# Attention loop: two PSUM banks for the accumulated heads, one for the turned probabilities, and the own block one step later

## The reference

```python
x = x + _L0_cond_ref(...)          # a 32x32 matrix per sequence, chosen by an index
x = x + _L1_cond_ref(...)          # base weight, bias and a LoRA adapter per sequence
x = x + _L2_cond_ref(...)          # attention, below
x = x + _L3_cond_ref(...)          # as the first
# _L2: HQ=32 query heads, HK=8 key heads, D=128, cache of L=512 keys per sequence
q, k, v = x @ Wq.T, x @ Wk.T, x @ Wv.T ; q, k = rope(rmsnorm(q)), rope(rmsnorm(k))
k_all = concat(k_cache[block_table], k)      # 512 + 32 keys
v_all = concat(v_cache[block_table], v)
probs = softmax(where(valid, q @ k_all.T * SCALE, -1e30))
return (probs @ v_all) @ Wo.T
```

## Time and profile before

| | |
|---|---|
| Time, median of 3 runs | 2406.7 us (2405.97 to 2408.63) |
| Span of the profiled execution | 2408.5 us (the core was busy from the first to the last instruction; nothing lies around it) |
| TensorE busy, matmuls | 2319.6 us, 96% of the span |
| TensorE weight loads | 2006.1 us, 83% |
| VectorE | 1763.3 us, 73% |
| ScalarE | 1629.7 us, 68% |
| GpSimd | 1411.4 us, 59% |
| Granted TensorE clock, mean | 0.994 of full speed |

### The profile page before, as it was taken

The page is one execution under the profiler, slowest core; times in us unless marked ns, Lnnn a source line. Parts: engine busy times, 40 slices in busy tenths (PEclk is TensorE's granted clock), DMA queues, the critical chain, the costliest instruction groups (busy, mean ns, idle before and its releaser), DMA issues.

```text
span 2408.5 us, 57141 instructions
## 1 busy us (share of the span) xinstructions
PE 2319.6 (96%) x14624; PEld 2006.1 (83%) x14624; DVE 1763.3 (73%) x5422; ACT 1629.7 (68%) x4605; POOL 1411.4 (59%) x2250
## 2 busy tenths in 40 slices
PE   8999999999998899999999999999999999998999
PEld 5778888888887788888888888888888888887777
DVE  3435777777778887887887887887887887886332
ACT  4324666666667887887887887887877877876221
POOL 1003444444447787887877877877877877872000
PEclk9999999999998999999999999999999999999999
DMA  4335333333348677876867867767767767775332
GB/s 162 95 110 165 98 101 102 117 98 101 101 120 265 207 239 221 257 231 220 262 226 226 260 226 229 255 223 236 251 223 234 251 219 241 248 220 191 109 131 100
DMA packets 347958, 455.94 MB, mean 189 GB/s; under 512 B 34506, under 2 KB 280842, under 8 KB 343695
## 3 DMA queue, kind: packets, MB, share of 16 engines
q1 hardware_dynamic: 308398, 315.83, 41.6%
q0 software_dynamic: 36864, 134.23, 17.0%
q10 hardware_dynamic: 2528, 4.29, 0.5%
HBM read 374.53 MB, written 79.69 MB: 189 GB/s over the span
## 4 chain that ended last, share of the span: by engine, by line
PE 65%; POOL 15%; issue 10%; ACT 6%; DVE 2%; DMA 1%; POOLq 0%; ACTq 0%; SPq 0%; DVEq 0%
PE S L1168 22%; PE bank L1236 8%; PE S L1251 7%; PE S L1209 7%; PE bank L1251 7%; PE bank L1092 7%; POOL k_lo L281 5%; POOL q_hi L546 4%; POOL regK L511 4%; POOL q_lo L548 3%; PE S L1122 2%; ACT regC L720 2%; PE bank L1245 2%; ACT regC L762 1%; ACT regC L756 1%
## 5 line engine op out<-in xcount | busy, mean ns | idle before, releaser
L1236 PE MATMUL bank<-regC,regK 128*128 128x128 f32 x4096 | 548.7, 277 | 31.9 <-DVE oT_lo L992 24.4
L1236 PEld LDWEIGHTS bank<-regC,regK 128*128 128x128 f32 x4096 | 507.4, 192 | 56.8 <-DVE oT_lo L992 36.0
L974 DVE CUSTOM_DVE_ANT_0 regC<-S,mask 128x544 f32<-128x544 f32 x512 | 367.8, 718 | 143.9 <-issue 139.1
L714 ACT CAST k_hi<-regK 128x544 fp32r<-128x544 f32 x512 | 330.4, 645 | 183.6 <-PE S L1209 165.2
L1092 PE MATMUL bank<-ident,regC 128*128 128x128 f32 x2688 | 409.3, 275 | 12.7 <-DVE regC L986 9.1
L720 ACT ACTIVATE regC<-regC,nmx 128x544 f32<-128x544 f32 x512 | 384.7, 751 | 44.7 <-DVE nmx L974 31.8
L1092 PEld LDWEIGHTS bank<-ident,regC 128*128 128x128 f32 x2688 | 320.8, 140 | 110.4 <-issue 66.9
L531 POOL TENSOR_TENSOR regC<-regC 128x256 f32<-128x256 f32 x320 | 244.4, 785 | 277.9 <-DVE regC L943 277.9
L546 POOL TENSOR_TENSOR q_hi<-regC,ones 128x128 fp32r<-128x128 f32 x512 | 262.5, 513 | 223.5 <-PE S L1209 219.8
L943 DVE SCALAR_TENSOR_TENSOR regC<-S,rstd,regK 128x128 f32<-128x128 f32 x1280 | 345.9, 343 | 16.7
L281 POOL TENSOR_TENSOR k_lo<-regK,k_hi 128x192 fp32r<-128x192 f32 x512 | 342.3, 669 | 12.6 <-ACT k_hi L714 12.6
(11 more groups left out here) (124 smaller groups left out, 3934.9 us busy)
## 6 DMA issues: line engine op xcount, KB each, us to landing
regK<-kT_cache SPq DMA_DIRECT2D x1024, 128.0 KB
qkT_d<-regC SPq DMA_DIRECT2D x160, 256.0 KB, 2.3
regC<-qkT_d SPq DMA_DIRECT2D x64, 512.0 KB
oT_d<-regC SPq DMA_DIRECT2D x64, 256.0 KB
regK<-oT_d SPq DMA_DIRECT2D x16, 1024.0 KB, 5.5
regC<-wqk SPq DMA_DIRECT2D x10, 1024.0 KB, 5.4
v_d<-regC SPq DMA_DIRECT2D x32, 256.0 KB, 2.3
regK<-qkT_d SPq DMA_DIRECT2D x64, 128.0 KB
```

The lines of the kernel that those rows point to most:

```text
L974: nc.vector.tensor_tensor_reduce(out=p_sb[u % 4], in0=scores[u % 2], in1=mask[u // HK % 2][:], scale=-SCALE, scalar=3e38, op0=ALU.add, op1 ...
L1236: last = nc.tensor.matmul(oP[:, j * P:(j + 1) * P], v_sb[b][:, m, u % HK * D:(u % HK + 1) * D], pT_sb[u % 2][:, m * P:(m + 1) * P], start= ...
```

## The change

Bank 4 alone holds the turned probabilities. Banks 5 and 6 hold the accumulated heads: first quads of a sequence in `oP[0]`, second quads in `oP[1]`. With that,

- the first `values` of a quad waits until the quad before the last has left its bank, not the last one;
- `turn_p(u)` waits for the copy of unit u-1 (`s_evA` at n, before n-1), and in step 4k for the own block's copies (`s_evB`);
- the own block's transpose moves on TensorE from the end of step 4k-1's `turn_p` (`turn_p` of the quad's last unit) to the head of step 4k, ahead of `score`, and waits there for the copy of unit 4k-1;
- its four copies move on ScalarE from behind that copy, ahead of `exps` in step 4k-1, to the head of step 4k, behind that `exps`.

The number of instructions stays, and no DMA is moved.

```diff
-        pT, oP, yP = bank[4:6], bank[6], bank[7]
+        pT, oP, yP = bank[4], bank[5:7], bank[7]
...
 (ScalarE, out_heads)
-                                   oP.rearrange("p (r s) -> p r s", s=C)).then_inc(s_ohi, 1)
+                                   oP[0].rearrange("p (r s) -> p r s", s=C)).then_inc(s_ohi, 1)
...
-                    nc.scalar.copy(o_st, oP).then_inc(s_ost, 1)
+                    nc.scalar.copy(o_st, oP[1]).then_inc(s_ost, 1)
+
+            def own_turned(g, u):
+
+                act.wait_ge(s_tb, g * HK + u // 4)
+                ge(act, s_po, g * HK + (u // 4 - 1))
+                for r in range(4):
+                    rows = slice(r * C, (r + 1) * C)
+                    last = nc.scalar.copy(pTo_sb[rows, r * P:(r + 1) * P], pT[rows, 0:P])
+                last.then_inc(s_evB, 1)
...
 (ScalarE, step)
+                if u % 4 == 0 and not (fixed and n == 0):
+                    own_turned(g, u)
                 if not (fixed and n + 4 >= NU):
                     split_k(n + 4, u + 4, g * 2 + (u + 4) // (2 * HK))
...
-                nc.scalar.copy(pT_sb[u % 2], pT[u % 2]).then_inc(s_evA, 1)
-                if u % 4 == 3:
-                    act.wait_ge(s_tb, g * HK + (u // 4 + 1))
-                    ge(act, s_po, g * HK + u // 4)
-                    for r in range(4):
-                        rows = slice(r * C, (r + 1) * C)
-                        last = nc.scalar.copy(pTo_sb[rows, r * P:(r + 1) * P], pT[0][rows, 0:P])
-                    last.then_inc(s_evB, 1)
+                nc.scalar.copy(pT_sb[u % 2], pT).then_inc(s_evA, 1)
...
 (VectorE, out_low: oP becomes oP[0])
...
 (TensorE, turn_p)
-                ge(pe, s_evA, n - 1)
-                transposes(pT[u % 2], p_sb[u % 4]).then_inc(s_ta, 1)
-                if u % 4 == 3:
-                    pe.wait_ge(s_evA, n)
-                    nc.tensor.transpose(pT[0][:, 0:P], po_sb[u // 4 % 2], ident[:]).then_inc(s_tb, 1)
+                if u % 4:
+                    ge(pe, s_evA, n)
+                else:
+                    ge(pe, s_evB, g * HK + u // 4)
+                transposes(pT, p_sb[u % 4]).then_inc(s_ta, 1)
+
+            def turn_own(g, u):
+
+                pe.wait_ge(s_evA, g * UG + u)
+                nc.tensor.transpose(pT[:, 0:P], po_sb[(u - 4) // 4 % 2], ident[:]).then_inc(s_tb, 1)
...
 (TensorE, values)
+                    ge(pe, s_oev, g * BT + u // HK)
+                elif j == 0:
                     ge(pe, s_ost, g * BT + u // HK)
-                elif j == 0:
-                    pe.wait_ge(s_oev, g * BT + (u // HK + 1))
                 pe.wait_ge(s_evA, n + 1)
+                to = oP[u // 4 % 2]
...
 (TensorE, step)
+                if u % 4 == 0 and not (fixed and n == 0):
+                    turn_own(g, u)
                 if not (fixed and n + 2 >= NU):
                     score(n + 2, u + 2)
```

More of the change, by code:

```diff
@@ L782, in _ @@
             for u in range(ROT):
-                if u == 3:
+                if u == 4:
                     act.wait_ge(s_ones, 6)
@@ L794, in _ @@
                 step(NT - 1, u)
+            own_turned(NT - 1, UG)
             out_heads(NT - 1, UG)
@@ L991, in out_low @@
                 at = slice(b * C, (b + 1) * C)
-                nc.vector.tensor_tensor(oT_lo.rearrange("p (r n) -> p r n", n=P)[:, :, at], oP.rearrange("p (r s) -> p r s", s=C),
+                nc.vector.tensor_tensor(oT_lo.rearrange("p (r n) -> p r n", n=P)[:, :, at], oP[0].rearrange("p (r s) -> p r s", s=C),
                                         oT_hi.rearrange("p (r n) -> p r n", n=P)[:, :, at].bitcast(F32), ALU.subtract)\
@@ L1228, in values @@
                     pe.wait_ge(s_v[b], pair * 64 + 64)
+                    ge(pe, s_oev, g * BT + u // HK)
+                elif j == 0:
                     ge(pe, s_ost, g * BT + u // HK)
-                elif j == 0:
-                    pe.wait_ge(s_oev, g * BT + (u // HK + 1))
                 pe.wait_ge(s_evA, n + 1)
+                to = oP[u // 4 % 2]
                 for m in range(4):
-                    last = nc.tensor.matmul(oP[:, j * P:(j + 1) * P], v_sb[b][:, m, u % HK * D:(u % HK + 1) * D],
+                    last = nc.tensor.matmul(to[:, j * P:(j + 1) * P], v_sb[b][:, m, u % HK * D:(u % HK + 1) * D],
                                             pT_sb[u % 2][:, m * P:(m + 1) * P],
@@ L1244, in values @@
                     at = u // 4 % 2 * D
-                    nc.tensor.matmul(oP, vo_sb[b][:, at:at + D], pTo_sb, start=False, stop=True).then_inc(s_po, 1)
+                    nc.tensor.matmul(to, vo_sb[b][:, at:at + D], pTo_sb, start=False, stop=True).then_inc(s_po, 1)
             def split_product(dst, o, w, h, first, last):
@@ L1301, in _ @@
                 step(NT - 1, u, None)
+            turn_own(NT - 1, UG)
             values(NT - 1, UG - 1)
```

## The result

The median over four runs is 2437.4 us (2436.4 to 2437.9), beside 2407.7 us (2406.0 to 2408.7) for the kernel before, run on the same chip. The ratio is 1.0123, with a 95% interval of 1.0108 to 1.0137: the change costs 1.2%, 29.7 us. The profiled execution has a span of 2436.0 us (before 2408.5).

The account below looks back on a forecast made before the run. No single engine bounds: TensorE's order and ScalarE hand-overs decide outside two GpSimd stretches. Steps 25 and 29 (8.5 us) plus 1, 5, 9 and 17 (20.1) add 28.6 us; on a 2408.5 us span, less 1.8: 2435 us, range 2414 to 2446.

Parts of the forecast that it names:

- two signs of being wrong: Step 25 taking no longer than 2.50 us from own matmul to values, or GpSimd's 14.5 us stretch changing over 0.3 us.
- Behind an L731: Behind the heads' copy L731, the probabilities' copy L756 ends about 0.2 us before oT_lo; values' wait shrinks by that.
- Steps 25, 1, 5: +0.29, +0.30, +0.22.: In these steps of a 32-step round TensorE's transposes start later by these us, waiting for the probabilities' copy.
- Step 9: +0.53.: First values in step 9 of the round start 0.53 us later, with ScalarE running exps before the own copies.
- ScalarE's wait for nmx ahead of exps(4k+2) gone.: On ScalarE, the 0.35 us wait for nmx before these exponentials goes, but starting exps late gives back as much.
- Step 29: +0.24.: First values in step 29 start 0.24 us later; the one place on the chain where the oT_lo wait went.
- Steps 13 and 21 under GpSimd's cover.: First values about 0.24 us later each, but costing nothing because TensorE waits for GpSimd in steps 16 and 24.
- In sum over 30 us: Transposes' waits for ScalarE's probabilities' copy: 0.3 to 0.6 us in up to eight places a round, over 30 us summed.
- The move priced at a loss in steps 9 and 29.: Own copies moved behind exps on ScalarE, priced within step 9's +0.53 us and step 29's +0.24 us.
- The rival in which nothing replaces the wait: Probabilities' copy ends before TensorE reaches step 4k+1's transposes; 16 us saved, 2391 us; chance 0.08.
- the one in which GpSimd hides it: GpSimd's stretches cover most of the attention loop, so gains and losses vanish: 2405 to 2411 us; chance 0.11.
- the one in which every quad pays in full: Covered quads leak and the later own matmul shows; eight quads pay 0.4 us, 51 us in all, 2458; chance 0.08.

Follow-up runs that it names:

- the spread kernels: Kernel before, changed kernel and the move alone, each with GpSimd's four gathers in steps 0, 2, 4, 6 instead of 2 to 5: 2403.8, 2423.1, 2402.8 us.
- the move alone: Against the kernel before, only the own block's transpose and copies one step later; two probability banks, one heads bank: 2403.9 us, ratio 0.9986.

## Why the prediction was right, and where it wasn't

The time, 2437.4 for 2435, and the mechanism were right: the heads' wait is replaced by the transposes' wait for L767. Of the two signs of being wrong neither came: step 25 takes 2.83 us from own matmul to values, for 2.50 before and 2.79 forecast, and GpSimd's stretch is 14.45 us (1446.20 to 1460.65) for 14.49. Of its steps:

- *"Behind an L731 it ends about 0.2 us before oT_lo lets values go. The wait shrinks by 0.2 us; it doesn't go."* With the transposes waiting for the same copy even that 0.2 isn't earned, as the kernel with one head bank shows.
- *Steps 25, 1, 5: +0.29, +0.30, +0.22.* Measured +0.29, +0.30, +0.21. The hand-over from the copy to a transpose, which no row had shown, is 0.15 us for the 0.14 taken. Step 17 has +0.21 for +0.29; the 0.12 of step 13, which lies ahead of the same wait for GpSimd, makes up for it in the sum. As the spread kernels show, the +0.29 of steps 17 and 25 is true only against a kernel before that has GpSimd's bursts. The term was right and its reason incomplete.
- *Step 9: +0.53.* Measured +0.67. The failed part is "its maximum is read out only at 1406.13": I took the time of the old trace over. In the changed kernel the read-out comes 6.69 us after oT_lo starts (1411.84 to 1418.53), before 6.19 (1399.86 to 1406.05): one maximum starts 0.26 us after its reciprocal (1414.64 to 1414.90), for 0.08 before, and the normalisation behind it takes 0.76 (1415.70) for 0.47 (1403.62). VectorE stands still 0.1 us at most in between. Moving L1004 away gives 0.61 back, nearly all of step 9's loss and not only the 0.14 above the forecast.
- *ScalarE's wait for nmx ahead of exps(4k+2) gone.* It is gone there, and has gone up to 0.68 us ahead of exps(4k+1), which now stands first. The prediction said nothing of this second place.
- *Step 29: +0.24.* Measured +0.02. Two terms were mis-sized. The step from the start of exps to that of the own copies takes 0.75 (1470.54 to 1471.29), not 0.87: the small own copies follow an exps sooner than the heads' copy does, from which I had the 0.87. So the values start 0.13 later in their interval, not 0.24. And the next score follows the values by 0.81 us (1475.46 to 1476.27), where it was 0.92 (1461.84 to 1462.76): values that start behind a wait take 1.16, those of now 1.06. I had priced up to the start of the values and not up to the next score.
- *Steps 13 and 21 under GpSimd's cover.* +0.12 and +0.01. The waits for k_lo in steps 16 and 24 shrank only by 0.1 us (0.54 and 0.67, for 0.63 and 0.77), not by 0.2 to 0.3.
- *"In sum over 30 us" of waits of L1097 for L756.* The list has 18.6 us. The delay is there, the entries aren't: four of eight lie under the modelled end of a score.
- *The move priced at a loss in steps 9 and 29.* Alone it gains 4.1 us: step 9 takes 0.02 less than before. Its order costs only together with the single bank, where step 9 grows by 0.69, and I had priced it as a term of its own.

So that the sum is so near, 28.6 us for 29.7, is partly luck, from errors that cancel: 0.22 and 0.08 too much in steps 29 and 17, 0.14 and 0.12 too little in steps 9 and 13. The rival in which nothing replaces the wait is refuted, the one in which GpSimd hides it too, the one in which every quad pays in full is refuted for the change as made; from the move alone to the changed kernel every quad does pay, but 0.16 to 0.69 us.

The Trainium skill ("Perfetto Trace Analysis", Matmuls) wants matmul groups rotated through banks. Here the rule, read for the probabilities, agrees with the trace: 33.5 us between one and two banks. Read for the heads it does not: 0, beside a single bank for the probabilities.

## What to carry to other kernels

When a scarce buffer is to be given to one of two tiles, compare what releases each: the second buffer is worth something only where its wait ends later than every other wait of the same instruction, and here the tile that turns over every step needed it more than the one that turns over every fourth. Before an edit is priced on one engine, look at how much slack the engines behind it have: here swapping two copies on ScalarE shortened three steps by 0.28 us each and lengthened three others by up to 0.58, where the transposes waited for VectorE. A stretch under another engine's bound not only hides delays: here it also let ScalarE catch up, and the steps behind it looked better than the same steps do without it. And a price read in one schedule holds for that schedule: the single bank cost 33.5 us in one and 20.2 in another that differed only in when GpSimd issued its gathers.

## What the runs showed of the hardware

- From the end of a ScalarE copy to the first transpose that reads past it, or to the values, it took 0.14 to 0.15 us wherever the lines above show such a wait, in the kernel before, the changed one and two variants.
- Where four transposes start behind the wait for the copy, their span as the profile models it is 0.63 us for 0.60, and the values start 0.46 or 0.47 behind them for 0.43. Where the eight value passes start behind a wait, their span is 1.13 or 1.16 for 1.06, and the next score starts 0.89 or 0.92 behind them (1410.63 to 1411.52 and 1461.84 to 1462.76 in the kernel before) for 0.81. In these traces the wait was cheaper ahead of the transposes.
- The same 128x512 normalisation on VectorE (L991) takes 0.47 or 0.48 us when GpSimd pauses or has just ended (1418.68, 1420.40 in the changed kernel) and 0.88 when GpSimd's k_lo runs beside it (1423.84). Where the normalisation started 0.11 us ahead of GpSimd's q_lo, q_lo took 0.68 for 0.46 (1429.17).
